# A scan's last 64 state channels in six TensorE passes instead of ten: weight halves side by side, sums added afterwards

## The chip, the cores and the metric

The kernel runs on one core of one Trainium2 chip. The metric is the device time of one execution in microseconds (us). Three runs of the kernel before took 5264.43, 5264.77 and 5265.05 us; the median is 5264.77 us.

## The reference, cut to what matters

A feature map x of 16 images, 56 by 56 positions, 192 channels, goes through two residual blocks. The first one concerns us: the group-normalized map is cut into 7x7 windows, normalized per token (layer norm 1), and run through a linear recurrence over the 49 tokens of each window; its states are mixed, normalized again (layer norm 2), and sent through a two-layer MLP with a GELU between.

```python
xB = xw @ Bm                      # xw: windows x 49 tokens x 192 channels
def step(h, xb):
    h = xb + h @ A                # A: 192 x 192
    return (h, h)
_, hs = jax.lax.scan(step, h0, swapaxes(xB, 0, 1))
w = swapaxes(hs, 0, 1) @ Cm
y = _ln(w, ln2_w, ln2_b)
y = gelu(y @ W1 + b1) @ W2 + b2   # W1: 192 x 768, W2: 768 x 192
x = x + w + y
```

The second block is windowed attention. It follows when the first block is done and the change does not touch it.

## The kernel before, in words

**Precision.** A float32 product is made of products of a narrower type: each operand is split into an upper part, rounded to that type, and a lower part, the remainder. The class `Split` (L81 on) holds four tiles for one weight matrix: `a_hi`, `a_lo` for input channels 0 to 127 and `b_hi`, `b_lo` for input channels 128 to 191. The b tiles have those 64 rows twice, because the data's second half keeps its upper part in partitions 0 to 63 and its lower part in partitions 64 to 127. So one product with 192 input channels is five matmuls (`Split.terms`): a_hi with upper and lower data, a_lo with upper data, b_hi and b_lo with both.

**Stages.** A preamble reads x for the group statistics and prepares the weights (L164 on ScalarE writes the upper parts, L176 on GpSimd the lower ones). Then comes the scan stage with the first block; then the attention.

**The scan stage.** It has 98 steps: 49 window positions (t) by two chunks (c) of 4 x 128 windows. Every engine runs the same `slot(t, c)` with its own part, several steps at once. With n = 2t + c, in slot n

- SyncE (SP) issues the load of x for step n+2 into `xt` (L352), then waits until `s_x1` says that the first block's output of step n-1 is complete (L360), and issues its 14 stores (L380). SP issues everything in this order, one after the other.
- TensorE (PE) does the scan of step n+1 (L619: `ps_h` gets ten passes for channels 0 to 127, then ten for channels 128 to 191, 512 columns each), the transposes of y of step n (L590, L592), the second half of the MLP's second layer of step n-1 (L604), the first MLP layer of step n (L635; it waits for the lower parts of y through `s_yl`), the mixing with C of step n+1 (L646), the transposes of the normalized x of step n+2, and the first half of the second layer of step n (L604).
- ScalarE (ACT) writes the upper parts of h (L402, two instructions, bias included), of y (L391, L392), the GELU (L416), the upper parts of the hidden layer (L421) and of xn.
- VectorE (DVE) starts its slot with group norm on `xt` for step n+2 (L501, L503), and waits there for the load. Then it writes the lower parts of h of step n+1 (L482, two instructions), the lower parts of y of step n (L480, two), and adds the second half of the MLP's output of step n-1 into x1 (L489, L492), which gives `s_x1`. The rest of the slot follows: statistics, g_lo, normalizations, the first half of x1.
- GpSimd (POOL) makes the residual, two powers, two of the g_lo pieces and the running sums.

Within one engine the order is written out by hand; across engines there are only semaphores. The head of the DVE slot, whose order matters below, is

```python
dve.wait_ge(s_x[c], 16 * (t + 2))
dve.tensor_tensor(xn[c][:, :, :], xt[c][:, :, :], R1[:, r, :], ALU.mult).then_inc(s_gs, 1)
dve.tensor_tensor(xn[c][:, :, :], xn[c][:, :, :], M1[:, r, :], ALU.subtract).then_inc(s_gn, 1)
dve.wait_ge(s_hh, n + 2)
lower_parts(h_hi[1 - c], h_lo[1 - c], ps_h, hbias).then_inc(s_hl, 1)
dve.wait_ge(s_yh, n + 1)
lower_parts(y_hi, y_lo, ps_g).then_inc(s_yl, 1)
dve.wait_ge(s_w2, n)
x1_half(1 - c, 1, s_xb, n).then_inc(s_x1, 1)
```

Of the kernel before, what the change touches and what calls it, by code (L numbers as in the profile page):

```python
# [8 lines left out]
f32r = mybir.dt.float32r  # L9
ALU = mybir.AluOpType  # L10
ACT = mybir.ActivationFunctionType
# [3 lines left out]
IMGS, SIDE, C = 16, 56, 192  # L15
# [8 lines left out]
P = 128  # L24
CB = C - P
# [4 lines left out]
NTOK = TPC * P  # L30
# [25 lines left out]
def build(nc, x, A, Bm, Cm, ln1, ln2, W1, b1, W2, b2,  # L56
# [3 lines left out]
    def sem(name):  # L60
        return top.enter_context(nc.semaphore(name))

    with top:
# [17 lines left out]
        class Split:  # L81
# [1 line left out]

            def __init__(self, ctx, name, cols):
                self.parts = [ctx.enter_context(nc.sbuf_tensor(f"{name}_{k}", [P, cols], f32r))
                              for k in ("a_hi", "a_lo", "b_hi", "b_lo")]

            def terms(self, data_hi, data_lo, cols, pick=lambda t: t):  # L90

# [5 lines left out]
        with ExitStack() as ctx:  # L97
            def sb(name, shape, dt=fp32, where=ctx):
                return where.enter_context(nc.sbuf_tensor(name, shape, dt))
# [3 lines left out]

            R1 = sb("R1", [P, NT, C])
            M1 = sb("M1", [P, NT, C])
            W_B, W_A, W_C = (Split(ctx, name, C) for name in ("wB", "wA", "wC"))
            W_1 = Split(ctx, "w1", HID)
            w2 = sb("w2", [P, FT, 2, C], f32r)
            b2b = sb("b2b", [P, C])
# [1 line left out]
            hbias = sb("hbias", [P, 2])  # L111
# [4 lines left out]
            with ExitStack() as pre:  # L116
# [14 lines left out]
                ps_g, ps_h = ps("ps_g0", [P, 512], where=pre), ps("ps_h0", [P, 512], where=pre)  # L131
# [18 lines left out]
                @block.scalar  # L150
                def _(act):
                    for dst, src in ((ident[:, :], identity), (img_mean[:, :], image_mean),
                                     (raw_2[:, :, :], W2.rearrange("(f p) n -> p f n", p=P)),
                                     (b2b[:, :], b2.partition_broadcast(P)),
                                     (l1[:, :, :], ln1), (l2[:, :, :], ln2), (b1c[:, :], b1)):
                        act.dma_start(dst, src).then_inc(s_w, 16)
                    for raw, src in ((raw_B, Bm), (raw_A, A), (raw_C, Cm), (raw_1, W1)):
                        act.dma_start(raw[:, :, :], src.rearrange("(k p) n -> p k n", p=P)).then_inc(s_w, 16)

                    act.wait_ge(s_fold, 1)  # L160
                    for full, parts in ((fold_B, W_B), (raw_A, W_A), (raw_C, W_C), (fold_1, W_1)):
                        for t in range(2):
                            act.activation(parts.parts[2 * t][:, :], full[:, t, :], ACT.Copy)
                    act.activation(w2[:, :, 0, :], raw_2[:, :, :], ACT.Copy).then_inc(s_wh, 1)  # L164

                @block.gpsimd
                def _(pool):
                    pool.memset(acc_x[:, :, :], 0.0)
                    pool.memset(acc_x2[:, :, :], 0.0)
                    pool.memset(neg_half[:, :], -0.5).then_inc(s_i0, 1)  # L170
                    pool.wait_ge(s_i0, 1)

                    pool.wait_ge(s_wh, 1)
                    for full, parts in ((fold_B, W_B), (raw_A, W_A), (raw_C, W_C), (fold_1, W_1)):
                        for t in range(2):
                            pool.tensor_tensor(parts.parts[2 * t + 1][:, :], full[:, t, :],  # L176
                                               parts.parts[2 * t][:, :], ALU.subtract)
                    pool.tensor_tensor(w2[:, :, 1, :], raw_2[:, :, :], w2[:, :, 0, :], ALU.subtract)

                    pool.wait_ge(s_fold, 11)  # L180
                    pool.tensor_tensor(gtab[:, 0, :, :], gvar[:, :, :],
                                       neg_half[:, :].rearrange("p (a b) -> p a b", a=2), ALU.pow).then_inc(s_pow, 1)
# [96 lines left out]
            xn_lo = [sb(f"xn_lo{b}", [P, NTOK], f32r) for b in range(2)]  # L279
            h_hi = [sb(f"h_hi{b}", [P, 2, NTOK], f32r) for b in range(2)]  # L280
            h_lo = [sb(f"h_lo{b}", [P, NTOK], f32r) for b in range(2)]
            yb = sb("yb", [P, TPC, C])
            y_hi, y_lo = sb("y_hi", [P, 2, NTOK], f32r), sb("y_lo", [P, NTOK], f32r)
            gF = [sb(f"gF{b}", [P, NTOK]) for b in range(4)]
# [28 lines left out]
            s_st1, s_ag1, s_ve1 = sem("ln1_stats"), sem("ln1_aggregated"), sem("ln1_var_eps")  # L313
            s_rs1, s_xn = sem("ln1_rstd"), sem("xn_ready")
            s_t1, s_xh, s_xl = sem("xn_transposed"), sem("xn_hi_ready"), sem("xn_lo_ready")
            s_scan, s_hh, s_hl = sem("scan_summed"), sem("h_hi_ready"), sem("h_lo_ready")
            s_cm, s_res, s_rsum = sem("mixed"), sem("residual_ready"), sem("residual_summed")
            s_st2, s_ag2, s_ve2 = sem("ln2_stats"), sem("ln2_aggregated"), sem("ln2_var_eps")
            s_rs2, s_y = sem("ln2_rstd"), sem("y_ready")
# [66 lines left out]
            @block.scalar  # L386
            def _(act):
                act.wait_ge(s_init, 1)

                def upper_parts(hi, full):  # L390
                    act.activation(hi[:, 0, :], full[:, 0, :], ACT.Copy)  # L391
                    return act.activation(hi[0:CB, 1, :], full[0:CB, 1, :], ACT.Copy)  # L392

                def slot(t, c):
                    n = CHUNKS * t + c
                    if there(n + 1):

                        d = 1 - c
                        act.wait_ge(s_scan, n + 2)
                        upto(act, s_cm, n)  # L400
                        for k, rows in enumerate((P, CB)):
                            last = act.activation(h_hi[d][0:rows, k, :], ps_h[0:rows, k, :], ACT.Identity,  # L402
                                                  bias=hbias[0:rows, k:k + 1])
                        last.then_inc(s_hh, 1)
                    if there(n):
                        act.wait_ge(s_t2, n + 1)
                        upper_parts(y_hi, ps_g).then_inc(s_yh, 1)
                    if there(n):
                        for f in range(FT):
                            act.wait_ge(s_w1, FT * n + f + 1)  # L410
                            if f == 0:
                                upto(act, s_w2, n)
                            elif f >= 4:

                                act.wait_ge(s_gld, len(LO_DVE) * n + LO_DVE.index(f - 4) + 1)
                            act.activation(gF[f % 4][:, :], ps_g[:, f % 2, :], ACT.Gelu,  # L416
                                           bias=b1f[:, f:f + 1]).then_inc(s_gelu, 1)

                            for g in range(max(f - 1, 0), f + (f == FT - 1)):
                                act.wait_ge(s_gelu, FT * n + g + 1)  # L420
                                act.activation(g_hi[:, g, :], gF[g % 4][:, :], ACT.Copy).then_inc(s_gh, 1)  # L421
                    if there(n + 2):
                        act.wait_ge(s_t1, n + 3)
                        upto(act, s_scan, n + 1)
                        upper_parts(xn_hi[c], ps_h).then_inc(s_xh, 1)

                slots(act, slot)
# [44 lines left out]

            @block.vector
            def _(dve):
                def lower_parts(hi, lo, full, bias=None):

                    for k, rows, dst in ((0, P, lo[:, :]), (1, CB, hi[CB:P, 1, :])):
                        src, up = full[0:rows, k, :], hi[0:rows, k, :]
                        if bias is None:
                            last = dve.tensor_tensor(dst, src, up, ALU.subtract)  # L480
                        else:
                            last = dve.scalar_tensor_tensor(out=dst, in0=src, scalar=bias[0:rows, k:k + 1], in1=up,  # L482
                                                            op0=ALU.add, op1=ALU.subtract)
                    return last

                def x1_half(b, half, partial, count):
# [7 lines left out]
                def slot(t, c):  # L494
# [9 lines left out]
                                          ALU.subtract).then_inc(s_gn, 1)  # L504
                    if there(n + 1):

                        dve.wait_ge(s_hh, n + 2)
                        lower_parts(h_hi[1 - c], h_lo[1 - c], ps_h, hbias).then_inc(s_hl, 1)
                    if there(n):
                        dve.wait_ge(s_yh, n + 1)  # L510
                        lower_parts(y_hi, y_lo, ps_g).then_inc(s_yl, 1)
# [72 lines left out]
            def _(pe):  # L584
# [23 lines left out]
                def slot(t, c):  # L608
                    n = CHUNKS * t + c
                    if there(n + 1):  # L610

                        d = 1 - c
                        pe.wait_ge(s_xl, n + 2)
                        upto(pe, s_hl, n)
                        for m, rows in enumerate((P, CB)):
                            cols = slice(P * m, P * m + rows)
                            terms = (*W_B.terms(xn_hi[d], xn_lo[d], cols), *W_A.terms(h_hi[d], h_lo[d], cols))
                            for k, (w, v) in enumerate(terms):
                                last = pe.matmul(ps_h[0:rows, m, :], w, v, start=(k == 0), stop=(k == len(terms) - 1))  # L619
                        last.then_inc(s_scan, 1)  # L620
                    if there(n):
                        pe.wait_ge(s_y, n + 1)
# [703 lines left out]
```

## Time and profile before

| | |
|---|---|
| runs of the kernel | 5264.43, 5264.77, 5265.05 us |
| span of the profiled execution, first to last instruction | 5261.6 us |
| median of the runs less this span | 3.2 us |
| preamble | up to about 160 us |
| scan stage, first to last L619 matmul | 167 to 2382 us |
| steps in the scan stage | 98 |

The profile is of one execution; its own time is its span of 5261.6 us and about 3 us around it, as the runs have. Times in rows are us from the span's start unless marked ns. PE is TensorE's matmuls, PEld its weight loads, SPq SyncE's queue, which issues the DMAs.

### The profile page before, as it was taken

To read this page: it belongs to the slowest core of one execution; us is meant where nothing else is said; L and a number is where in the kernel's file an instruction comes from. 1 tells how busy PE (TensorE), PEld (TensorE's weight loads), DVE (VectorE), ACT (ScalarE), POOL (GpSimd) and SP (SyncE) were. 2 spreads that over 40 slices of the span, in tenths; PEclk is the share of its full clock that TensorE was granted. 3 is DMA by queue.
4 is the path that set the end of the run, shared out by engine and by line. 5 is a ranking of instruction groups with operands and counts; after the bars stand their busy time and mean duration, and the time that the engine had idled before them with its cause. 6 is when DMAs were issued, how large, how long until landed. Compare 5 with 4: busy or idle time off the path is not lost.

```text
span 5261.6 us, 134580 instructions
## 1 busy us (share of the span) xinstructions
PE 5043.1 (96%) x48584; PEld 4492.2 (85%) x48584; DVE 4296.8 (82%) x8359; ACT 2931.9 (56%) x5618; POOL 2646.9 (50%) x1717
## 2 busy tenths in 40 slices
PE   0699999999999999996999999999999999999999
PEld 0588888888888888885999999999999999999998
DVE  6788888888888888884777777777777777777777
ACT  0244444444444444442766666666666666666666
POOL 0245555555545554554555555555555555555554
PEclk9999999999999999997999999999999999999999
DMA  7011111111111111111111111111111111111111
GB/s 309 26 38 39 39 41 38 39 39 40 41 37 39 39 41 38 39 39 43 35 37 36 38 39 36 36 36 36 39 37 36 39 38 36 36 36 37 39 36 32
DMA packets 254250, 233.59 MB, mean 44 GB/s; under 512 B 19836, under 2 KB 252492, under 8 KB 253004
## 3 DMA queue, kind: packets, MB, share of 16 engines
q1 hardware_dynamic: 251460, 230.74, 14.8%
q10 hardware_dynamic: 2736, 2.14, 0.1%
q8 instruction: 33, 0.54, 0.0%
q14 instruction: 21, 0.16, 0.0%
HBM read 145.48 MB, written 87.33 MB: 44 GB/s over the span
## 4 chain that ended last, share of the span: by engine, by line
PE 53%; DMA 0%; DVE 0%; POOL 0%; ACT 0%; issue 0%; SPq 0%; ACTq 0%; DVEq 0%
PE ps_s L1195 18%; PE ps_t L1205 8%; PE ps_w L1143 7%; PE ps_w L1175 7%; PE ps_w L1156 5%; PE ps_v L1233 5%; PE ps_w L1130 2%; DMA mask<-in_shift_mask 0%; PE ps_s L1112 0%; PE ps_s L1113 0%; POOL E L860 0%; DVE L L1067 0%; DVE mx L1071 0%; DVE bias L1017 0%; DVE sm L1075 0%
## 5 line engine op out<-in xcount | busy, mean ns | idle before, releaser
L860 POOL TENSOR_TENSOR E<-E,ri 128x588 f32<-128x588 f32 x512 | 809.5, 1581 | 1271.3 <-DVE ri L1077 1271.3
L1195 PE MATMUL ps_s<-Kp,Qm 128*64 128x98 f32 x12288 | 1001.6, 250 | 0.0
L1195 PEld LDWEIGHTS ps_s<-Kp,Qm 128*64 128x64 f32 x12288 | 903.4, 135 | 67.2 <-issue 49.8
L945 ACT ACTIVATE PT<-ps_t 128x768 f32<-128x768 f32 x512 | 414.0, 809 | 643.2 <-PE ps_t L1205 643.2
L1067 DVE SCALAR_TENSOR_TENSOR L<-ps_s,bias 128x588 f32<-128x588 f32 x512 | 394.3, 770 | 408.3 <-PE ps_s L1195 408.2
L604 PE MATMUL ps_o<-w,g_hi 128*128 128x384 f32 x2352 | 709.9, 365 | 5.9 <-DVE g_lo L544 4.1
L416 ACT ACTIVATE gF<-ps_g,b1f 128x512 f32<-128x512 f32 x588 | 404.9, 689 | 394.0 <-PE ps_g L635 391.8
L604 PE MATMUL ps_o<-w,g_lo 128*128 128x192 f32 x2352 | 534.4, 254 | 0.0
L402 ACT ACTIVATE h_hi<-ps_h,hbias 128x512 fp32r<-128x512 f32 x196 | 123.1, 679 | 702.6 <-PE ps_h L619 702.6
L443 POOL TENSOR_TENSOR res<-xt,b2b 128x768 f32<-128x768 f32 x98 | 180.8, 1845 | 591.1 <-DVE x L492 591.1
L604 PEld LDWEIGHTS ps_o<-w,g_hi 128*128 128x128 f32 x2352 | 429.1, 189 | 26.6 <-issue 24.8
L1205 PE MATMUL ps_t<-ident,E 128*128 128x128 f32 x3072 | 447.7, 282 | 0.8 <-POOL E L860 0.7
L604 PEld LDWEIGHTS ps_o<-w,g_lo 128*128 128x128 f32 x2352 | 443.4, 191 | 0.0
L1071 DVE TENSOR_REDUCE mx<-L 128x12 f32<-128x588 f32 x512 | 392.1, 766 | 17.6
L1175 PE MATMUL ps_w<-wp,oT 128*128 128x192 f32 x2048 | 388.3, 333 | 0.7 <-ACT oT L964 0.7
L1075 DVE TENSOR_REDUCE sm<-E 128x12 f32<-128x588 f32 x512 | 386.2, 754 | 0.0
L1205 PEld LDWEIGHTS ps_t<-ident,E 128*128 128x128 f32 x3072 | 326.7, 140 | 63.4 <-POOL E L860 1.7
L1080 DVE TENSOR_TENSOR L<-L,mx 128x588 f32<-128x588 f32 x512 | 362.1, 707 | 0.0
L936 ACT ACTIVATE E<-L 128x588 f32<-128x588 f32 x512 | 357.7, 699 | 4.0 <-DVE L L1080 0.7
L421 ACT ACTIVATE g_hi<-gF 128x512 fp32r<-128x512 f32 x588 | 355.3, 621 | 0.0
L453 POOL TENSOR_TENSOR g_lo<-gF,g_hi 128x512 fp32r<-128x512 f32 x196 | 250.5, 1298 | 198.5 <-ACT g_hi L421 198.5
L1175 PEld LDWEIGHTS ps_w<-wp,oT 128*128 128x128 f32 x2048 | 326.3, 190 | 9.3 <-ACT oT L964 0.8
(208 smaller groups left out, 13082.4 us busy)
## 6 DMA issues: line engine op xcount, KB each, us to landing
xs<-in_x SPq DMA_DIRECT2D x8, 4704.0 KB, 22.6
xt<-in_x SPq DMA_DIRECT2D x98, 384.0 KB, 3.4
x_cells<-x SPq DMA_DIRECT2D x784, 48.0 KB
xb<-x_cells SPq DMA_DIRECT2D x256, 147.0 KB
out<-yo SPq DMA_DIRECT2D x256, 147.0 KB
gnr<-gn_rows SPq DMA_DIRECT2D x128, 192.0 KB
x_cells<-x SPq DMA_DIRECT2D x392, 24.0 KB
x_cells<-x SPq DMA_DIRECT2D x196, 3.0 KB
```

Source lines behind the costliest of these rows:

```text
L416: act.activation(gF[f % 4][:, :], ps_g[:, f % 2, :], ACT.Gelu, bias=b1f[:, f:f + 1]).then_inc(s_gelu, 1)
L604: last = pe.matmul(dst, g[:, f, P * k:P * (k + 1)], w, start=(f == 0 and i == 0), stop=(f == FT - 1 and i == 1))
L860: pool.tensor_tensor(e, e, ri[p][:, :].unsqueeze(2).to_broadcast([P, HEADS, T]), ALU.mult)\
L945: act.activation(PT[lp % 2][:, :, :].rearrange("p (a b) q -> p a (b q)", a=2), ps_t[:, :, 0:JB * P], ACT.Copy).then_inc(s_ptc, 1)
L1067: dve.scalar_tensor_tensor(out=L[p][:, :, :].rearrange("p (a h) m -> p a (h m)", a=2), in0=ps_s[:, :, 0:HEADS // 2 * T], scalar=HD ** -0.5 ...
L1071: dve.tensor_reduce(mx[p][:, :], L[p][:, :, :], AX.X, ALU.max).then_inc(s_mx, 1)
L1075: dve.tensor_reduce(sm[pp][:, :], E[pp][:, :, 0:T], AX.X, ALU.add).then_inc(s_sm, 1)
L1080: dve.tensor_tensor(L[p][:, :, :], L[p][:, :, :], mx[p][:, :].unsqueeze(2).to_broadcast([P, HEADS, T]), ALU.subtract).then_inc(s_sub, 1)
L1143: last = pe.matmul(ps_w(QK + m)[:, 0:NW * TE].rearrange("p (w t) -> p w t", t=TE), w, x, start=(k == 0), stop=(k == len(terms) - 1))
L1175: last = pe.matmul(ps_w(OUT1 if half else OUT0)[:, C * a:C * (a + 1)], oT[d][p][:, k, :, :].rearrange("p w t -> p (w t)"), wp[:, k, :], st ...
L1195: last = pe.matmul(ps_s[SLOT * w:SLOT * (w + 1), j // JB, 2 * T * (j % JB):2 * T * (j % JB + 1)], Qm[c][:, j, 2 * p + w, :], Kp[c][:, j // ...
L1205: last = pe.transpose(ps_t[:, j // JB, P * (j % JB):P * (j % JB + 1)], E[lp][:, 2 * j:2 * j + 2, :].rearrange("p h m -> p (h m)"), ident[: ...
```

## The change

The scan's second group of output channels, 128 to 191, used 64 of the 128 columns of the stationary operand. Now the tiles `a_hi` and `b_hi` of B and A get 64 more columns, into which the lower weight parts of these channels are written as well. A pass with columns 128 to 255 of such a tile gives the product with the upper weights in partitions 0 to 63 of `ps_h[:, 1]` and that with the lower weights in partitions 64 to 127. `packed_terms` lists three passes per matrix instead of five, so there are 10 + 6 passes in a step instead of 10 + 10.

The two halves must be added, and one instruction reads the accumulators of both halves at different partitions, so it goes by steps: ScalarE copies the lower half to `h_low` in SBUF; VectorE adds the upper half, bias and `h_low` into `h_b`; ScalarE rounds `h_b` to the upper part of h; VectorE makes the lower parts. Two semaphores are new: `s_hc` (h_low copied) and `s_hb` (h_b summed).

```diff
-            W_B, W_A, W_C = (Split(ctx, name, C) for name in ("wB", "wA", "wC"))
+            W_B, W_A = (Split(ctx, name, C, CB) for name in ("wB", "wA"))
+            W_C = Split(ctx, "wC", C)
...
+            def packed_terms(self, data_hi, data_lo):
+                both = slice(self.cols - self.beside, self.cols + self.beside)
+                a_hi, _, b_hi, _ = self.parts
+                return ((a_hi[:, both], data_hi[:, 0, :]), (a_hi[:, both], data_lo[:, :]), (b_hi[:, both], data_hi[:, 1, :]))
...
                     for full, parts in ((fold_B, W_B), (raw_A, W_A), (raw_C, W_C), (fold_1, W_1)):
                         for t in range(2):
-                            pool.tensor_tensor(parts.parts[2 * t + 1][:, :], full[:, t, :],
-                                               parts.parts[2 * t][:, :], ALU.subtract)
+                            pool.tensor_tensor(parts.lower(t), full[:, t, :], parts.upper(t), ALU.subtract)
+                            if parts.beside:
+                                pool.tensor_tensor(parts.lower_beside(t), full[:, t, P:C], parts.upper(t)[:, P:C],
+                                                   ALU.subtract)
...
                         act.wait_ge(s_scan, n + 2)
                         upto(act, s_cm, n)
-                        for k, rows in enumerate((P, CB)):
-                            last = act.activation(h_hi[d][0:rows, k, :], ps_h[0:rows, k, :], ACT.Identity,
-                                                  bias=hbias[0:rows, k:k + 1])
-                        last.then_inc(s_hh, 1)
+                        act.activation(h_low[0:CB, :], ps_h[CB:P, 1, :], ACT.Copy).then_inc(s_hc, 1)
+                        act.activation(h_hi[d][:, 0, :], ps_h[:, 0, :], ACT.Identity, bias=hbias[:, 0:1])
+                        act.wait_ge(s_hb, n + 2)
+                        act.activation(h_hi[d][0:CB, 1, :], h_b[0:CB, :], ACT.Copy).then_inc(s_hh, 1)
...
+                        d = 1 - c
+                        dve.wait_ge(s_hc, n + 2)
+                        dve.scalar_tensor_tensor(out=h_b[0:CB, :], in0=ps_h[0:CB, 1, :], scalar=hbias[0:CB, 1:2],
+                                                 in1=h_low[0:CB, :], op0=ALU.add, op1=ALU.add).then_inc(s_hb, 1)
                         dve.wait_ge(s_hh, n + 2)
-                        lower_parts(h_hi[1 - c], h_lo[1 - c], ps_h, hbias).then_inc(s_hl, 1)
+                        dve.scalar_tensor_tensor(out=h_lo[d][:, :], in0=ps_h[:, 0, :], scalar=hbias[:, 0:1],
+                                                 in1=h_hi[d][:, 0, :], op0=ALU.add, op1=ALU.subtract)
+                        dve.tensor_tensor(h_hi[d][CB:P, 1, :], h_b[0:CB, :], h_hi[d][0:CB, 1, :],
+                                          ALU.subtract).then_inc(s_hl, 1)
...
-                        for m, rows in enumerate((P, CB)):
-                            cols = slice(P * m, P * m + rows)
-                            terms = (*W_B.terms(xn_hi[d], xn_lo[d], cols), *W_A.terms(h_hi[d], h_lo[d], cols))
+                        first = slice(0, P)
+                        for m, terms in enumerate(((*W_B.terms(xn_hi[d], xn_lo[d], first),
+                                                    *W_A.terms(h_hi[d], h_lo[d], first)),
+                                                   (*W_B.packed_terms(xn_hi[d], xn_lo[d]),
+                                                    *W_A.packed_terms(h_hi[d], h_lo[d])))):
                             for k, (w, v) in enumerate(terms):
-                                last = pe.matmul(ps_h[0:rows, m, :], w, v, start=(k == 0), stop=(k == len(terms) - 1))
+                                last = pe.matmul(ps_h[:, m, :], w, v, start=(k == 0), stop=(k == len(terms) - 1))
                         last.then_inc(s_scan, 1)
```

## Rows read from the trace of the kernel before

**Rows 1.** The page: span, busy us, share of the span, instructions of each engine.

```profile
span 5261.6 us, 134580 instructions
...
PE 5043.1 (96%) x48584; PEld 4492.2 (85%) x48584; DVE 4296.8 (82%) x8359; ACT 2931.9 (56%) x5618; POOL 2646.9 (50%) x1717
```

**Rows 2.** Waits of 400 to 2290 us, SP's queue too: us, times, longest.

```profile
DVE xn L501 <- DMA xt<-in_x: 74.9, 83, 1.2
...
SPq L360 <- DVE x L492: 779.0, 83, 9.4
```

**Rows 3.** Timeline of SP's queue: start us, us, engine, line, what.

```profile
1033.68 0.43 SPq L352 DMA_DIRECT2D xt<-in_x  x1
1044.60 11.28 SPq L380 DMA_DIRECT2D x_cells<-x  x14
1056.59 0.44 SPq L352 DMA_DIRECT2D xt<-in_x  x1
```

**Rows 4.** Timeline of DVE, head of one slot; in brackets idle before and releaser.

```profile
1036.98 1.39 DVE L501 TENSOR_TENSOR xn<-xt,R 128x768 f32<-128x768 f32 x1 [0.71 <-DMA xt<-in_x]
1038.40 0.96 DVE L503 TENSOR_TENSOR xn<-xn,M 128x768 f32<-128x768 f32 x1
1039.37 0.75 DVE L482 SCALAR_TENSOR_TENSOR h_lo<-ps_h,hbias,h_hi 128x512 fp32r<-128x512 f32 x1
1040.13 0.74 DVE L482 SCALAR_TENSOR_TENSOR h_hi<-ps_h,hbias,h_hi 64x512 fp32r<-64x512 f32 x1
1040.91 0.69 DVE L480 TENSOR_TENSOR y_lo<-ps_g,y_hi 128x512 fp32r<-128x512 f32 x1
1041.62 0.68 DVE L480 TENSOR_TENSOR y_hi<-ps_g,y_hi 64x512 fp32r<-64x512 f32 x1
1042.39 0.56 DVE L489 TENSOR_TENSOR x<-ps_o,res 128x384 f32<-128x384 f32 x1
1042.98 0.56 DVE L492 TENSOR_TENSOR x<-ps_o,x 128x384 f32<-128x384 f32 x1
```

**Rows 5.** Timeline of PE in the same step: scan's narrow passes, last L604, first L635.

```profile
1035.60 0.39 PE L619 MATMUL ps_h<-xn_hi,wB_a_hi 128*64 128x512 f32 x1
...
1037.65 0.39 PE L619 MATMUL ps_h<-h_hi,wA_b_lo 128*64 128x512 f32 x1
...
1041.99 0.36 PE L604 MATMUL ps_o<-w,g_hi 128*128 128x384 f32 x1
1042.36 0.50 PE L635 MATMUL ps_g<-y_hi,w_a_hi 128*128 128x512 f32 x1
```

**Rows 6.** PEld groups of 400 to 2290 us: busy us, mean ns, then idle before.

```profile
L635 PEld LDWEIGHTS ps_g<-y_hi,w_a_hi 128*128 128x128 f32 x498 | 93.1, 187 | 44.9 <-DVE y_hi L480 20.9
...
L619 PEld LDWEIGHTS ps_h<-xn_hi,wB_a_hi 128*128 128x128 f32 x83 | 15.9, 192 | 0.0
```

**Rows 7.** Timeline of ACT in the same step.

```profile
1038.08 1.25 ACT L402 ACTIVATE h_hi<-ps_h,hbias 128x512 fp32r<-128x512 f32 x2 [7.14 <-PE ps_h L619]
1039.23 0.58 ACT L391 ACTIVATE y_hi<-ps_g 128x512 fp32r<-128x512 f32 x1
1039.71 0.59 ACT L392 ACTIVATE y_hi<-ps_g 64x512 fp32r<-64x512 f32 x1
1043.82 0.69 ACT L416 ACTIVATE gF<-ps_g,b1f 128x512 f32<-128x512 f32 x1 [3.52 <-PE ps_g L635]
```

**Rows 8.** ACT groups of 400 to 2290 us: busy us, mean ns, then idle before.

```profile
L421 ACT ACTIVATE g_hi<-gF 128x512 fp32r<-128x512 f32 x498 | 300.9, 621 | 0.0
...
L402 ACT ACTIVATE h_hi<-ps_h,hbias 64x512 fp32r<-64x512 f32 x83 | 55.7, 671 | 0.0
...
L392 ACT ACTIVATE y_hi<-ps_g 64x512 fp32r<-64x512 f32 x83 | 48.5, 584 | 0.0
```

**Rows 9.** The source view of L176 on POOL (min/median/max ns), and a wait of the whole span.

```profile
L176 POOL TENSOR_TENSOR wB_a_lo<-fold_B,wB_a_hi x1: 589/589/589, 94.7 to 94.7; 128x192 fp32r<-128x192 f32 x1
...
POOL gtab L181 <- DVE gvar L228: 39.5, 1, 39.5
```

**Rows 10.** Stretches at the scan's start: busy us of PE, PEld, DVE, ACT, POOL, then PEclk.

```profile
172.00:178.80 6.80, 3.91 (x25) 2.66 (x23) 2.96 (x10) 1.25 (x2) 0.00 (x0) 1.00 0.00 0
178.80:189.10 10.30, 6.65 (x24) 5.26 (x23) 7.54 (x23) 1.07 (x2) 3.79 (x3) 0.50 0.14 41
```

**Rows 11.** Timeline of PE there: the one long wait within the first stretch.

```profile
177.26 0.36 PE L646 MATMUL ps_r<-wC_a_hi,h_hi 128*128 128x192 f32 x1 [2.89 <-DVE h_hi L482]
```

More of the change, by code:

```diff
@@ L81, in build, with __init__, upper, lower @@
         class Split:
-            def __init__(self, ctx, name, cols):
-                self.parts = [ctx.enter_context(nc.sbuf_tensor(f"{name}_{k}", [P, cols], f32r))
+            def __init__(self, ctx, name, cols, beside=0):
+                self.cols, self.beside = cols, beside
+                self.parts = [ctx.enter_context(nc.sbuf_tensor(f"{name}_{k}", [P, cols + beside * (k[-1] == "i")], f32r))
                               for k in ("a_hi", "a_lo", "b_hi", "b_lo")]
+            def upper(self, t):
+                return self.parts[2 * t][:, 0:self.cols]
+            def lower(self, t):
+                return self.parts[2 * t + 1][:, :]
+            def lower_beside(self, t):
+                return self.parts[2 * t][:, self.cols:self.cols + self.beside]
+            def packed_terms(self, data_hi, data_lo):
+                both = slice(self.cols - self.beside, self.cols + self.beside)
+                a_hi, _, b_hi, _ = self.parts
+                return ((a_hi[:, both], data_hi[:, 0, :]), (a_hi[:, both], data_lo[:, :]), (b_hi[:, both], data_hi[:, 1, :]))
             def terms(self, data_hi, data_lo, cols, pick=lambda t: t):
@@ L162, in _ @@
                         for t in range(2):
-                            act.activation(parts.parts[2 * t][:, :], full[:, t, :], ACT.Copy)
+                            act.activation(parts.upper(t), full[:, t, :], ACT.Copy)
                     act.activation(w2[:, :, 0, :], raw_2[:, :, :], ACT.Copy).then_inc(s_wh, 1)
@@ L281, in build @@
             h_lo = [sb(f"h_lo{b}", [P, NTOK], f32r) for b in range(2)]
+            h_low, h_b = sb("h_low", [P, NTOK]), sb("h_b", [P, NTOK])
             yb = sb("yb", [P, TPC, C])
@@ L315, in build @@
             s_t1, s_xh, s_xl = sem("xn_transposed"), sem("xn_hi_ready"), sem("xn_lo_ready")
-            s_scan, s_hh, s_hl = sem("scan_summed"), sem("h_hi_ready"), sem("h_lo_ready")
+            s_scan, s_hc, s_hb, s_hh, s_hl = sem("scan_summed"), sem("h_b_low_copied"), sem("h_b_summed"), sem("h_hi_ready"), sem("h_lo_ready")
             s_cm, s_res, s_rsum = sem("mixed"), sem("residual_ready"), sem("residual_summed")
@@ L474, in _, with lower_parts @@
             def _(dve):
-                def lower_parts(hi, lo, full, bias=None):
+                def lower_parts(hi, lo, full):
                     for k, rows, dst in ((0, P, lo[:, :]), (1, CB, hi[CB:P, 1, :])):
[L478 to L483, printed above, removed]
+                        last = dve.tensor_tensor(dst, full[0:rows, k, :], hi[0:rows, k, :], ALU.subtract)
                     return last
```

## Prediction

> **What bounds the kernel now.** The page comes first: TensorE is busy 96% of the span, VectorE 82% [rows 1]. That reads as a kernel bound by its matmuls, of which the change removes some. But busy shares cannot tell a full engine from one that is paced by something of nearly the same length, so I read who waits for whom in the steady part of the scan stage. There VectorE begins every slot by waiting for the load of x, 74.9 us in 83 steps or 0.90 us a step; no other wait appears at its slot's head. SyncE in turn waits 779.0 us for VectorE's L492 before it may store [rows 2]. These two waits face each other, and the timeline shows that they form a ring.
>
> Follow one turn. SyncE issues the load at 1033.68 [rows 3]; VectorE starts L501 at 1036.98, 3.30 us later. It then runs L501, L503, the two lower parts of h, the two of y, L489 and L492 with gaps under 0.1 us and ends at 1042.98 + 0.56 = 1043.54 [rows 4]: 6.56 us. That end releases SyncE: the first store goes out at 1044.60, 1.06 us later, the 14 stores take 11.28 us, and 0.71 us behind them the next load is issued at 1056.59, because it stands behind them in the queue [rows 3]. 3.30 + 6.56 + 1.06 + 11.28 + 0.71 = 22.91 us, which is exactly the time between the two loads. Nobody in this ring waits for anybody outside it, but for at most 0.06 us before L489, where VectorE is free at 1042.30 and starts at 1042.39 [rows 4].
>
> TensorE turns with the ring, but it is the one that waits: before L635 its weight load waits 20.9 us in 83 steps for VectorE's lower part of y, 0.25 us a step [rows 6]. That lower part is a piece of the ring. So **the ring sets the step**, TensorE follows with little slack, and what the change does to VectorE between L503 and L492 counts in full.
>
> **The change, part by part.** *Four passes fewer.* The ten narrow passes start between 1035.60 and 1037.65 [rows 5]: 2.05 / 9 = 0.228 us apiece. A pass with 128 stationary columns needs a longer weight load, 192 ns [rows 6], still under the 228. Four passes less end the scan 0.91 us earlier in each step. In the ring this is worth nothing: the lower parts of h start when L503 ends, at 1039.36, and the upper parts were ready at 1038.08 + 1.25 = 1039.33 [rows 4, 7]. They would be ready earlier, and VectorE would still be in L503. The 0.91 us turn into a longer wait before L635. They also end L604 earlier, which takes away the 0.06 us before L489.
>
> *ScalarE's copy of h_low.* It starts at the scan's end and takes about 0.58 us like L392 [rows 8]. Here the earlier scan helps: it ends near 1037.2 instead of 1038.08, the copy near 1037.8, and L503 at 1039.36. Hidden by the wait for the load and by L501 and L503; with the cover gone it would cost its 0.6 us. L402 for channels 0 to 127 is hidden behind it in the same way.
>
> *VectorE's sum h_b.* A new instruction in the ring, of the form of the second L482 (64x512, one operand from PSUM): 0.74 us and 0.02 for the gap [rows 4].
>
> *The new round trip.* Behind h_b VectorE waits until ScalarE has rounded h_b; h_lo, which does not need it, stands behind the same wait. No row shows this 64x512 copy from SBUF. The nearest are 584 ns (64x512, from PSUM) and 621 ns (128x512, from SBUF) [rows 8]; I take 0.60, with 0.55 and 0.69 as ends (the latter is somewhat over the 671 of L402). A handover costs 0.06 us from VectorE (1042.30 to L635 at 1042.36 [rows 4, 5]) and 0.04 back (ScalarE's 1039.33 to 1039.37 [rows 4, 7]). Sum 0.70 us, between 0.60 and 0.90 if both handovers are doubled. Queued behind ScalarE's wait are the upper parts of y; they take 0.59 + 0.48 = 1.07 us [rows 7] and VectorE needs them only after h_lo and the lower part, 0.75 + 0.70 later than the handover. Hidden, by 0.4 us. The GELU behind them waits 3.52 us for TensorE anyway [rows 7].
>
> *h's lower part* becomes a plain subtraction, 0.68 like L480 for 0.74: minus 0.06 [rows 4].
>
> *Preamble.* Four subtractions on GpSimd, at most 0.59 us each as their wider sisters take; GpSimd later waits 39.5 us for VectorE [rows 9]. Nothing.
>
> No DMA is added or moved. Nothing else on the ring changes: L501 meets GpSimd's running sums as before, since both are paced from the same end of the lower y.
>
> **The sum.** 0.76 + 0.70 - 0.06 - 0.06 = 1.34 us a turn (1.24 to 1.54 with the ends). The load is waited for in 92 of the 98 steps (83 of them in the steady stretch, one each [rows 2]; the others are at the ends, where the shorter scan and the longer handover about cancel). 92 x 1.34 = 123 us on the span of 5261.6 [rows 1]; the runs lie 3.2 us above that span, so 5264.8 + 123 = **5388 us**. With the ends of the unknown: 5379 to 5406.
>
> **Rivals.** *TensorE's clock falls* (slower still). TensorE's wait before L635 grows to 0.25 + 0.91 + 1.34 = 2.5 us a step. Near the start of the stage it waited 2.89 us once, at full clock [rows 11], and 1.5 us after it resumed the granted clock went from 1.0 to 0.5, from 2.4 to 1.2 GHz, for 10.3 us [rows 10]. The Trainium skill ("TensorE: Matmul & The Clock Gate", section What's actually happening) says why: "the default state is throttled, and activity releases the throttle"; by that rule this longer wait can cost clock, and the trace agrees once, for a longer wait. Each L635 pass would then take about twice its 0.23 us for some 15 passes, so TensorE loses perhaps 1.7 us. VectorE has 0.90 us before the load lands to absorb it; 0.8 us would reach the ring. A late TensorE has a shorter wait in the next step, so I count every other step: 0.4 x 92 = 37 us, 5425 us. Against it: 2.5 is under 2.89, and no row shows such a wait at a steady pace.
>
> *TensorE paces after all* (faster). If the ring had 1.3 us of slack that the turn above hides, TensorE would set the step through its own chain: scan end, h, y, L635. Before, from 1038.04 to 1042.30, 4.26 us [rows 4, 5]. After: 0.62 (h_low) + 0.80 (h_b) + 0.64 + 0.77 + 0.70 + 0.71 + 0.70 = 4.94. So 0.68 longer for 0.91 saved, -0.23 x 98 = -23 us: 5242 us. It decides wherever the load lands 1.3 us before VectorE asks for it; all 83 waits say it lands late [rows 2].
>
> The Trainium skill ("Perfetto Trace Analysis", section Identifying the Most-Contended Engine) would have the engine with the highest occupancy taken as the bound, with weight-load share as TensorE's measure: 85% here, still the highest [rows 1]. By that rule all of 0.91 x 98 = 89 us is gained, 5176 us; the waits of rows 2 and 6 disagree, since TensorE is the one that waits.
>
> *The ring absorbs it* (same). If part of SyncE's 11.28 us were itself a wait for earlier transfers, a later start would shorten it by as much. The stores come out evenly and SyncE idles 9.4 us a step before them [rows 2], so little speaks for it: 5265 us.
>
> **How the numbers follow.** The ring with the clock kept 0.52, with a falling clock 0.34, TensorE pacing 0.07 (its pure form included), absorbed 0.05, and 0.02 for something slower that I don't see. Chances: faster 0.07, same 0.05, slower 0.88, where 0.2% of 5265 is about 10 us, what a measurement of this kernel can tell from no change. The range takes in both ring cases and their ends: 5370 (1.15 us a turn) to 5440.
>
> **What would show it.** Right: a step of about 24.1 us; VectorE still waiting about 0.9 us for the load in each; about 0.7 us a step of VectorE waiting for ScalarE's h_hi; TensorE's wait before L635 near 2.5 us; SyncE's stores still 11.3 us. Half-clock stretches after these waits would show the second case. Wrong: loads that land before VectorE asks, a step under 22.8 us, or stores issued faster.

## Result and profile after

The changed kernel takes **5520.9 us** (median of 4 runs, 5519.58 to 5525.6) against 5264.91 us (4 runs, 5264.43 to 5265.34) for the kernel before: a ratio of 1.0489, 95% interval 1.0475 to 1.0503. I had forecast 5388 us, with 5440 as the upper end. The direction is right; the size is 133 us short.

Lines have moved: L501 is now L517, L503 L519, L482 is h_b L525, h_lo L528 and h_hi L530, L480 L499, L489 and L492 are L505 and L508, L532 L555, L619 L644, L635 L660, L604 L627; SyncE's load is L373 and its stores L401. The page of the changed kernel, to be read beside [rows 1]:

```profile
span 5518.9 us, 133996 instructions
...
PE 5088.2 (92%) x48192; PEld 4570.3 (83%) x48192; DVE 4435.5 (80%) x8457; ACT 3000.1 (54%) x5716; POOL 2645.6 (48%) x1721
```

TensorE has 392 matmuls fewer (4 in each of 98 steps), yet is busy for longer, 5088 us for 5043. Less work in more busy time means that each matmul took longer. The windows say why; columns as in [rows 10], the last but two being the granted clock:

```profile
215.00:360.00 145.00, 132.48 (x790) 117.70 (x789) 127.32 (x266) 66.10 (x115) 68.72 (x48) 1.00 0.14 38
400.00:1400.00 1000.00, 913.19 (x5083) 802.09 (x5081) 846.93 (x1718) 432.46 (x745) 449.42 (x314) 0.93 0.13 35
1006.56:1009.30 2.74, 2.74 (x7) 2.16 (x8) 2.57 (x11) 0.20 (x1) 1.47 (x1) 0.50 0.00 0
```

From 215 to 360 us the scan runs at full clock, from 400 us on at a mean of 0.93: with two levels, 1.2 and 2.4 GHz, (1 - 0.93) / 0.5 is 14% of the time at the lower one, or some 3.6 us of each step of 25.60. The third row is one such stretch, and TensorE's timeline shows where it lies:

```profile
1006.56 0.79 PE L660 MATMUL ps_g<-y_hi,w_a_hi 128*128 128x512 f32 x1 [2.17 <-DVE y_hi L499]
1007.15 0.63 PE L660 MATMUL ps_g<-y_lo,w_a_hi 128*128 128x512 f32 x1
1007.58 0.63 PE L660 MATMUL ps_g<-y_hi,w_a_lo 128*128 128x512 f32 x1
...
1009.90 0.40 PE L660 MATMUL ps_g<-y_hi,w_b_hi 128*128 128x512 f32 x1
1010.14 0.40 PE L660 MATMUL ps_g<-y_hi,w_b_lo 128*128 128x512 f32 x1
```

TensorE waits 2.17 us for the lower part of y, and resumes at half clock: passes start 0.43 us apart (1007.15 to 1007.58), 0.24 later on. It is the start of the first MLP layer, on which ScalarE's GELU and VectorE's g_lo depend.

The waits of the steady stretch (400 to 2290 us, 74 steps; us, times, longest), SP's queue last:

```profile
DVE g_lo L555 <- ACT g_hi L442: 197.2, 146, 2.1
PEld ps_g L660 <- DVE y_hi L499: 183.5, 74, 2.5
...
SPq L381 <- DVE x L508: 902.6, 74, 12.2
```

VectorE's wait for the load, 0.90 us a step in [rows 2], is not among them. TensorE's wait before the first layer is 183.5 / 74 = 2.48 us, forecast near 2.5. The one that grew is at L555: 197.2 / 74 = 2.66 us a step, 1.13 at the same place (L532) of the kernel before, in the same stretch:

```profile
DVE g_lo L532 <- ACT g_hi L421: 94.1, 166, 0.7
```

SyncE idles 12.2 us a step for 9.4: its stores cannot be what grew. VectorE's slot head, beside [rows 4]:

```profile
1024.17 0.56 DVE L508 TENSOR_TENSOR x<-ps_o,x 128x384 f32<-128x384 f32 x1
1024.65 2.17 DVE L517 TENSOR_TENSOR xn<-xt,R 128x768 f32<-128x768 f32 x1
...
1027.73 0.74 DVE L525 SCALAR_TENSOR_TENSOR h_b<-ps_h,hbias,h_low 64x512 f32<-64x512 f32 x1
1029.17 0.75 DVE L528 SCALAR_TENSOR_TENSOR h_lo<-ps_h,hbias,h_hi 128x512 fp32r<-128x512 f32 x1 [0.70 <-ACT h_hi L425]
1029.93 0.69 DVE L530 TENSOR_TENSOR h_hi<-h_b,h_hi 64x512 fp32r<-64x512 f32 x1
```

h's part is as forecast: 0.74 for h_b, 0.70 for the round trip, 0.69 for the lower part. But L517 starts right behind L508 and takes 2.17 us (mean 2.12), 1.20 in the kernel before. GpSimd and SyncE's queue in the same step say why:

```profile
1022.34 1.86 POOL L487 TENSOR_TENSOR acc_x<-acc_x,x 128x768 f32<-128x768 f32 x1
1024.14 1.87 POOL L490 TENSOR_TENSOR acc_x<-acc_x,x1sq 128x768 f32<-128x768 f32 x1
```

```profile
1008.97 11.37 SPq L401 DMA_DIRECT2D x_cells<-x  x14
1020.60 0.43 SPq L373 DMA_DIRECT2D xt<-in_x  x1
```

The load goes out at 1020.60; with the 3.30 us of [rows 3, 4] it lands near 1023.9, before VectorE asks at 1024.65. So VectorE no longer waits, and L517 begins while GpSimd is still in the last of its sums (1024.14 to 1026.01). L517 ends at 1026.82, 0.81 us after that: about the 0.95 us that it takes where none of the sums runs beside it (e5 below).

The first steps of the same trace ran otherwise, as I had forecast them:

```profile
320.37 11.38 SPq L401 DMA_DIRECT2D x_cells<-x  x14
...
344.67 11.45 SPq L401 DMA_DIRECT2D x_cells<-x  x14
...
368.60 11.36 SPq L401 DMA_DIRECT2D x_cells<-x  x14
...
394.48 11.37 SPq L401 DMA_DIRECT2D x_cells<-x  x14
...
419.83 11.28 SPq L401 DMA_DIRECT2D x_cells<-x  x14
```

Up to 368.60 the steps are 24.3 and 23.9 us, behind it 25.9 and 25.4. **One execution shows the forecast step while the clock is full and the longer one once it falls.**

### The profile page after: what moved, and what is told of

Same layout as the page of the kernel before. It is cut to its first block, busy times and chain, and to the rows that moved or that the text cites. A ratio compares the mean times of both kernels' runs of the same rounds, so it can differ in the third digit from the quotient of the medians.

```text
span 5518.9 us, 133996 instructions
## 1 busy us (share of the span) xinstructions
PE 5088.2 (92%) x48192; PEld 4570.3 (83%) x48192; DVE 4435.5 (80%) x8457; ACT 3000.1 (54%) x5716; POOL 2645.6 (48%) x1721
## 4 chain that ended last, share of the span: by engine, by line
PE 50%; DMA 0%; DVE 0%; POOL 0%; ACT 0%; issue 0%; SPq 0%; ACTq 0%; DVEq 0%
PE ps_s L1220 17%; PE ps_t L1230 7%; PE ps_w L1168 7%; PE ps_w L1200 6%; PE ps_w L1181 5%; PE ps_v L1258 4%; PE ps_w L1155 2%; DMA mask<-in_shift_mask 0%; PE ps_s L1137 0%; PE ps_s L1138 0%; POOL E L885 0%; DVE L L1092 0%; DVE mx L1096 0%; DVE bias L1042 0%; DVE sm L1100 0%
## 5 line engine op out<-in xcount | busy, mean ns | idle before, releaser
L627 PE MATMUL ps_o<-w,g_hi 128*128 128x384 f32 x2352 | 710.0, 365 | 5.9 <-DVE g_lo L567 4.1
L627 PE MATMUL ps_o<-w,g_lo 128*128 128x192 f32 x2352 | 534.5, 254 | 0.0
L660 PE MATMUL ps_g<-y_hi,w_a_hi 128*128 128x512 f32 x588 | 280.3, 477 | 215.5 <-DVE y_hi L499 215.5
L627 PEld LDWEIGHTS ps_o<-w,g_hi 128*128 128x128 f32 x2352 | 429.3, 189 | 26.3 <-issue 24.4
L627 PEld LDWEIGHTS ps_o<-w,g_lo 128*128 128x128 f32 x2352 | 443.6, 191 | 0.0
L422 ACT ACTIVATE h_low<-ps_h 64x512 f32<-64x512 f32 x98 | 58.4, 596 | 613.5 <-PE ps_h L644 613.5
```

The lines of the kernel that those rows point to most:

```text
L627: last = pe.matmul(dst, g[:, f, P * k:P * (k + 1)], w, start=(f == 0 and i == 0), stop=(f == FT - 1 and i == 1))
```

## Experiments

A step is read from SyncE's load issues between 1000 and 2000 us of the profiled execution: first, last, and the steps between.

| kernel | us (interval of the ratio to before) | loads from, to, steps | step us |
|---|---|---|---|
| before | 5264.91 | 1011.02, 1990.98, 43 | 22.79 |
| changed | 5520.9 (1.0475 to 1.0503) | 1020.60, 1993.41, 38 | 25.60 |
| e1: changed, wait filled | 5392.18 (1.0223 to 1.0257) | 1008.71, 1997.46, 41 | 24.12 |
| e2: changed, four passes back | 5393.26 (1.0225 to 1.026) | 1010.69, 1999.70, 41 | 24.12 |
| e3: changed, load first | 5518.5 (1.0464 to 1.0499) | 1008.32, 1981.06, 38 | 25.60 |
| e4: before, load first | 5266.21 (0.999 to 1.0009) | 999.78, 1980.71, 43 | 22.81 |
| e5: changed, sums later | 5522.69 (1.0473 to 1.0508) | 1020.03, 1992.84, 38 | 25.60 |
| e6: changed, y first | 5314.46 (1.0076 to 1.0109) | 1003.79, 1984.49, 42 | 23.35 |
| e8: e6, load first, sums later | 5362.09 (1.0167 to 1.0201) | 1020.22, 1976.63, 40 | 23.91 |
| e9: before, the edits of e8 | 5295.67 (1.0039 to 1.0073) | 1011.46, 1983.13, 42 | 23.14 |
| e10: e6, h behind statistics | **5194.2** (0.9849 to 0.9882) | 1004.70, 1999.17, 45 | 22.10 |
| e11: before, the order of e10 | 5283.25 (1.0021 to 1.0047) | 1016.54, 1983.93, 42 | 23.03 |

### Does the clock make the difference? (e1, e2)

e1 fills TensorE's wait with ten passes whose result nobody reads; e2 puts the four saved passes back, as useless ones, at the head of the second scan group. Both add work to the changed kernel and take none away.

```diff
 pe (e1)
+    for _ in range(10):
+        pe.matmul(ps_r[:, 0, :], W_1.upper(0)[:, 0:P], ..., start=True, stop=True)
     pe.wait_ge(s_yl, n + 1)
 pe (e2), second group only
+    for w, v in terms[0:4]:
+        pe.matmul(ps_h[:, m, :], w, v, start=True, stop=True)
     for k, (w, v) in enumerate(terms):
```

> The changed kernel with ten useless passes of 512 columns (10 x 0.229 = 2.29 us) put where TensorE waits 2.2 us a step for the lower part of y. Clock theory: the wait is what halves TensorE's clock in every step; late first-layer passes make VectorE's slot late, and L517 late into GpSimd's sums. With the wait filled the granted clock in the scan stage stays 1.0, the load of x is again what VectorE waits for, and the step is 22.8 + 1.35: 5262 + 92 x 1.35 + 3 = about 5390 us, faster with more work. Rival, round trip alone: the clock is a companion, the added VectorE and ScalarE steps and the overlap with GpSimd make up the 256 us; then the time stays at 5521 us.

> The changed kernel with four useless passes at the head of the second group, so that TensorE's scan takes as long as before and only the round trip for h_b remains. Clock theory: the wait before the first layer shrinks from 2.5 to about 1.6 us; if such a wait still halves the clock, about 5500 us, if not, about 5390 us, which would say that the saved passes themselves cost 130 us. Round trip alone: 5521 us.

More work, 129 us and 128 us less time. The window and the waits of e1 (78 steps):

```profile
400.00:1400.00 1000.00, 1000.00 (x5814) 879.87 (x5813) 867.42 (x1827) 455.47 (x785) 477.84 (x333) 1.00 0.14 37
```

```profile
DVE g_lo L555 <- ACT g_hi L442: 93.8, 156, 0.8
DVE xn L517 <- DMA xt<-in_x: 61.4, 78, 1.1
DVE h_lo L528 <- ACT h_hi L425: 54.6, 78, 0.7
PEld ps_g L664 <- DVE y_hi L499: 25.8, 78, 0.4
```

and the group of its first product (busy us, mean ns, idle before):

```profile
L517 DVE TENSOR_TENSOR xn<-xt,R 128x768 f32<-128x768 f32 x78 | 101.3, 1298 | 61.4 <-DMA xt<-in_x 61.4
```

The clock is at 1.00 and the ring through the load is back. Its step is 24.12 us, 1.33 above the kernel before; the forecast's sum was 1.34. e2's scan also ran at 1.00, with this wait before the first layer:

```profile
PEld ps_g L662 <- DVE y_hi L499: 121.8, 78, 1.6
```

With 1.56 us in every step the clock stayed; with 2.48 us in every step it fell. So **the saved passes cost 128 us**: with them put back, even as useless ones, the wait is short enough here for the clock to stay.

How the 1.48 us between e1 and the changed kernel come about, from waits and groups of both: the wait at L555 grows from 93.8 / 78 = 1.20 to 2.66 us (+1.46, the first layer at half clock); the wait for the load goes (-0.79); L517 is stretched from 1.30 to 2.12 (+0.83). Sum 1.50. The slack ahead of the load absorbed half of the clock's cost, and the stretch beside GpSimd gave it back.

### Does the load still matter? (e3, e4)

SyncE issues the stores of a slot one slot later, behind the next load. e4 does the same to the kernel before.

```diff
 sp
-    if there(n - 1):
-        d, u = (1 - c), (t if c else t - 1)
+    if there(n - 2):
+        d, u = c, t - 1
         ...
-        sp.wait_ge(s_x1, n)
+        sp.wait_ge(s_x1, n - 1)
```

> The changed kernel with SyncE's stores issued one slot later, behind the load, so that the load of x no longer stands behind 14 stores. The prediction's ring of load and stores, if it still set the step: a gain of 100 us and more. Clock theory: in the changed kernel VectorE no longer waits for the load, so nothing moves: 5510 to 5530 us.

> The kernel before with the same edit. If the ring of load and stores alone set its step of 22.8 us, TensorE's work is next at about 22.4 us: 5265 - 96 x 0.4 = 5227 us. If VectorE's L501, started earlier, is stretched by GpSimd's running sums as in the changed kernel (2.1 for 1.2 us), the 0.9 us are given back: 5260 to 5270 us.

In the changed kernel almost nothing moves (2.4 us): the load's ring no longer sets its step. In the kernel before nothing moves either, and that speaks against my account of it. VectorE no longer waits for the load there, and its busy time rises from 885 to 923 of 1000 us; the group of e4's first product:

```profile
L502 DVE TENSOR_TENSOR xn<-xt,R 128x768 f32<-128x768 f32 x82 | 174.0, 2122 | 0.9
```

From 1.20 to 2.12 us: what VectorE had waited it now spends beside the sums. The kernel before had at least two rings of the same length, the load's and VectorE's own with a stretched first product. A third candidate is TensorE itself: its matmuls leave next to no gap in either kernel (busy 999.92 of 1000 us before, 999.81 in e4, from 400 to 1400 us), and neither run tells it from the rings.

### Is it the sums that stretch L517? (e5)

GpSimd's three sums wait until the next slot's L519 has run, so that none stands beside L517.

```diff
 pool
     pool.wait_ge(s_x1, n)
+    if there(n + 3):
+        pool.wait_ge(s_gn, n + 4)
```

> The changed kernel in which GpSimd starts its three running sums only when VectorE has done L519 of the next slot, so that they no longer run beside L517. Overlap theory: L517 falls from 2.12 to about 0.96 us; the clock still falls, so about 1.15 us of the 25.6 us step go and the time is near 5521 - 85 x 1.15 = 5420 us, with the load of x waited for again. Rival: L517 is slow for another reason (the load's data arriving beside it); it stays at 2.1 us and the time at 5521 us.

The groups of e5 (its lines are two further down):

```profile
L532 DVE TENSOR_TENSOR h_hi<-h_b,h_hi 64x512 fp32r<-64x512 f32 x74 | 136.7, 1847 | 1.0
...
L519 DVE TENSOR_TENSOR xn<-xt,R 128x768 f32<-128x768 f32 x74 | 70.6, 954 | 8.4 <-DMA xt<-in_x 7.8
```

The first product falls to 0.954 us, so the sums were its cause. But the sums now stand beside h_hi's difference, which rises from 0.685 to 1.847: 1.17 saved, 1.16 lost. h_b and h_lo between them stay at 0.74 and 0.75. Those read PSUM; the two that were stretched read both operands from SBUF. The Trainium skill ("SBUF — State Buffer", section Who interferes with whom) says the same: a VectorE instruction with two SBUF inputs contends with a GpSimd instruction that reads SBUF. The trace agrees, with these numbers.

### Can the order be mended? (e6, e8, e9)

y's lower parts first on VectorE, then h_b and the second half of x1, then h's lower parts (e6). e8 adds the edits of e3 and e5; e9 makes the edits of VectorE, SyncE and GpSimd on the kernel before, where ScalarE still writes h's upper parts ahead of y's.

```diff
 dve (e6)
+    lower_parts(y_hi, y_lo, ps_g)
     h_b = ps_h + bias + h_low
-    h_lo, h_hi lower parts
-    lower_parts(y_hi, y_lo, ps_g)
     x1_half(1 - c, 1, s_xb, n)
+    h_lo, h_hi lower parts
 act (e6)
+    upper_parts(y_hi, ps_g)
     h_hi[0:CB, 1] = h_b
-    upper_parts(y_hi, ps_g)
```

> The changed kernel with VectorE and ScalarE doing y first: only h_b stays between L519 and the second half of x1, h's lower parts come behind it. Ring theory: TensorE's wait before the first layer shrinks to well under 1 us, the clock stays at 1.0, and the step is set by VectorE's own slot with L517 at 2.1 us, some 22.4 us: 5230 us. If the clock alone mattered and the ring not, the time would be that of the filled wait, 5390 us.

> The changed kernel with y first, the stores one slot behind the load, and GpSimd's sums behind L519. Then nothing but TensorE's own work should set the step, 22.35 - 0.91 = 21.4 us: 5265 - 96 x 1.35 = about 5135 us. If VectorE's slot still sets it, 5200 us or more.

> The kernel before, ten and ten passes, with the same three edits. If TensorE sets the step in both, it is 22.35 us here and the time is 5265 - 96 x 0.4 = 5225 us, some 90 us more than with six passes; if VectorE or a transfer sets it, both kernels come out alike.

All three came out above what theory gave. e6 does take most of the loss back, and its clock stays at 1.00. But VectorE is then busy 960 of 1000 us, with these groups, and this wait of TensorE's transposes:

```profile
L518 DVE TENSOR_TENSOR xn<-xt,R 128x768 f32<-128x768 f32 x81 | 171.1, 2113 | 0.8
...
L541 DVE TENSOR_TENSOR h_hi<-h_b,h_hi 64x512 fp32r<-64x512 f32 x81 | 148.8, 1837 | 1.1
```

```profile
PEld ps_h L617 <- DVE xn L564: 115.0, 81, 1.5
```

h_hi's difference now runs beside GpSimd's residual and is stretched again, and with h_lo it stands ahead of the statistics of xn, so xn is late for TensorE. In e8 the same wait is 1.46 us a step, and a late scan delays y as well:

```profile
DVE y_lo L503 <- ACT y_hi L414: 131.0, 80, 2.8
PEld ps_h L620 <- DVE xn L567: 115.5, 79, 2.1
```

Part of its scan is at half clock (mean 0.98). In e9 VectorE's wait for y_hi alone is 176.5 / 82 = 2.15 us: it asks for y first, and ScalarE makes it behind h. My expectations had counted what each edit took off one path, and not what it moved onto another.

### A version that beats both (e10, e11)

h's two lower parts go behind the statistics, ahead of VectorE's first g_lo (L555): where VectorE stood idle for ScalarE, and GpSimd takes only its powers.

```diff
 dve (e10, on e6)
-    h_lo, h_hi lower parts
     bn_stats, bn_aggr, vea
+    h_lo, h_hi lower parts
     g_lo of LO_DVE[:2]
```

> The changed kernel with y's lower parts first on VectorE, h_b behind them, and h's lower parts behind the statistics of xn, just ahead of the first of VectorE's g_lo, where VectorE now stands idle 2.1 us for ScalarE and GpSimd has only the powers to take. Theory (the step is the ring through VectorE's slot: y's lower parts, first layer, GELU, g_lo, and back): with y first alone VectorE was busy 960 of 1000 us and h_hi's difference took 1.84 us beside GpSimd's residual; here it should fall back to about 0.69 us and stand in idle time, so a step of 22.3 to 22.8 us and 5220 to 5265 us, with the granted clock at 1.00 through the scan. Rival 1: the difference is only stretched somewhere else and xn is still late for TensorE's transposes (a wait of 1 to 2 us a step ahead of them): near the 5314 us of y first alone. Rival 2: h's lower parts are now late for the mix, which waits for them, and the clock falls again: above 5400 us.

> The same placing of h's lower parts in the kernel before: y's lower parts and the second half of x1 first, h's lower parts behind the statistics. Theory: the kernel before is held at 22.9 us by two rings of nearly one length (the load ring, and VectorE's slot with the stretched first product); this edit takes 1.4 us off the way from y to the load in both, so TensorE paces the step at about 22.4 us: 5215 to 5240 us. Rival 1: h_hi's difference or xn is late for TensorE, a wait ahead of the transposes or the mix takes the gain: 5265 to 5300 us. Rival 2: TensorE was the bound all along: 5262 to 5267 us.

e10 takes **5194.2 us, 0.9865 of the kernel before** (0.9849 to 0.9882), below what theory expected. The waits of e10, the group of h_hi's difference, its window and TensorE ahead of the first layer:

```profile
DVE xn L518 <- DMA xt<-in_x: 61.8, 86, 1.2
PEld ps_o L632 <- issue: 38.1, 86, 0.4
PEld ps_h L618 <- DVE xn L565: 10.1, 37, 0.3
```

```profile
L554 DVE TENSOR_TENSOR h_hi<-h_b,h_hi 64x512 fp32r<-64x512 f32 x85 | 58.2, 685 | 1.1
```

```profile
400.00:1400.00 1000.00, 989.80 (x5894) 881.48 (x5894) 939.82 (x1994) 500.87 (x864) 522.66 (x362) 1.00 0.15 40
```

```profile
1012.34 0.36 PE L632 MATMUL ps_o<-w,g_hi 128*128 128x384 f32 x1
1012.54 0.39 PE L665 MATMUL ps_g<-y_hi,w_a_hi 128*128 128x512 f32 x1
```

h_hi's difference is at 0.685 us, the wait for ScalarE ahead of the first g_lo, 2.66 us a step in the changed kernel, has no row in this list, and the first MLP layer (L665) follows the matmuls ahead of it without a gap. The waits of TensorE in this list make (38.1 + 10.1) / 86 = 0.56 us a step: it is nearly full. But VectorE waits for the load in every step again (61.8 / 86 = 0.72 us), and the load's ring closes, here from the load that SyncE issued at 1004.70:

```profile
1008.31 1.39 DVE L518 TENSOR_TENSOR xn<-xt,R 128x768 f32<-128x768 f32 x1 [0.70 <-DMA xt<-in_x]
...
1013.39 0.56 DVE L509 TENSOR_TENSOR x<-ps_o,x 128x384 f32<-128x384 f32 x1
```

```profile
1015.01 11.29 SPq L401 DMA_DIRECT2D x_cells<-x  x14
1027.00 0.44 SPq L373 DMA_DIRECT2D xt<-in_x  x1
```

That is 3.61 us to L518, 5.64 to the end of L509 with no gap over 0.04 us between VectorE's instructions, 1.06 to the first store, 11.29 for the stores and 0.70 to the next load: 22.30 us, the whole turn (22.10 in the mean). VectorE's part is shorter than the 6.56 us of [rows 4], since h's lower parts have left it. So the ring and TensorE have nearly the same length in e10; no run tells which of them holds it at 22.10.

e11 gives VectorE the same order in the kernel before, with all ten passes; ScalarE keeps its own there, h's upper parts ahead of y's. It became *slower* than the kernel before (theory had said 5215 to 5240). Its waits:

```profile
DVE y_lo L480 <- ACT y_hi L392: 80.5, 82, 1.0
DVE x L489 <- PE ps_o L604: 55.9, 82, 0.7
DVE xn L501 <- DMA xt<-in_x: 55.7, 82, 1.0
PEld ps_o L604 <- issue: 36.7, 82, 0.4
```

Two waits are new on VectorE: 0.98 us a step for y's upper part and 0.68 for TensorE's second layer ahead of x1. Both lie within the load's ring, which therefore waits for ScalarE and TensorE and doesn't hold the step by itself. TensorE waits 36.7 / 82 = 0.45 us a step at L604, and nowhere near as long anywhere else: with ten passes the matmuls fill nearly all of the 23.03 us, so the order could win little. The two kernels differ in step by 23.03 - 22.10 = 0.93 us, and in time by 89 us: the four passes at 0.228 us are 0.91 us a step and 89 us in 98. TensorE is busy 990 of 1000 us in e10 and 989 in e11, from 400 to 1400 us. **Where TensorE is nearly full, the saved passes are worth about all they cost.** VectorE's order alone gains nothing. What it would gain with y first on ScalarE too stays open, because e11 left that out.

## Why the prediction was wrong

*The direction and the ring.* h_b (0.76 forecast; 0.74 and a gap), the round trip (0.70; 54.6 / 78 = 0.70) and the shorter difference (0.68; 0.685) were right, and so was their sum as long as the clock stayed: 123 us forecast, 126 and 127 measured in e1 and e2 against the 5265.85 us of the kernel before, measured beside them, with 24.12 us for the "about 24.1" of a step. Four passes fewer bring the ring nothing: right, and TensorE's wait came out as forecast at 2.5.

*What failed* is the choice between that case and the rival "TensorE's clock falls", and above all that rival's price. I had its mechanism and place, and set against it that 2.5 us is under the 2.89 of [rows 11]. The clock fell all the same. Two of its terms were mis-sized:

- "I count every other step". After 368 us it fell in every step. The alternation was an argument without a row behind it: y is late in every step because VectorE's slot is long, and TensorE's lateness adds to that slot.
- "VectorE has 0.90 us before the load lands to absorb it". It did absorb 0.79 us, but the line "L501 meets GpSimd's running sums as before, since both are paced from the same end of the lower y" fell: once VectorE doesn't wait for the load, L517 starts beside the sums and takes 0.83 us longer. The rival's 1.7 us lost by TensorE measured 1.46 at L555; I let 0.8 reach the ring in half the steps, 0.4 us; 1.48 reached it in each.

0.4 x 92 = 37 us were forecast for the clock, 5520.9 - 5392.2 = 129 us measured (e1).

*"The ring sets the step, TensorE follows with little slack."* The first half is too strong. e4 takes the load out of the ring and leaves the time as it was; what else had the same length (VectorE's slot, TensorE's matmuls) could not be seen in a wait, because only the last of several releasers shows. That had no part in the miss, since y and h lie in both rings.

*"TensorE paces after all"* had 0.07 and its conditions were rightly judged unfulfilled here. e10 and e11 show what the matmuls are worth once the order brings TensorE close to full.

*The signs I had named.* SyncE's stores still took 11.3 us and the wait for h_hi was 0.7. The wait for the load, named as the sign of a right step, vanished: by my own list, "loads that land before VectorE asks" meant wrong.

## What to carry to other kernels

Work taken from an engine that waits anyway lengthens its wait, and on TensorE that wait can cost the clock in every step: fill the wait as a test, since a kernel that gets faster with useless matmuls has named its cause. Where several rings have nearly the same length, slack in one is not free: ask what the early instruction will then run beside. Before giving up a saving, look for a place in the order where the new instructions meet idle time of their engine and of its neighbour; here the same saving went from +4.9% to -1.3% by where three of VectorE's instructions (h_b and h's two lower parts) and ScalarE's copy of h_b stand.

## What the runs showed of the hardware

- A wait of TensorE of about 2.5 us in every step of 25.6 us came with half clock for a few us behind each; 1.56 us in every step (e2) did not. The length of the wait alone does not decide it. In the changed kernel's own first steps, 215 to 360 us, six such waits made 14.0 us, 2.3 each, and the clock stayed at 1.00. In e3 six waits made 14.9 us between 327 and 490 us, eight made 19.8 us between 494 and 700 us, 2.5 each in both stretches; the clock was full in the first and fell in the second:

```profile
327.20:490.00 162.80, 149.44 (x894) 132.94 (x894) 145.95 (x293) 74.67 (x130) 77.68 (x54) 1.00 0.14 38
494.50:700.00 205.50, 187.69 (x1043) 164.84 (x1042) 174.05 (x355) 89.03 (x153) 92.56 (x65) 0.93 0.13 35
```

  What else it takes, and why the fall begins only at about 368 us in the changed kernel, stays open. The Trainium skill ("TensorE: Matmul & The Clock Gate", section What's actually happening) has activity release the throttle, and the rows agree in the direction; what they add is that one wait of 2.5 us a step can cost the clock in every step.
- The changed kernel, e3 and e5 have the same step of 25.60 us to two decimals between 1000 and 2000 us, though L517 takes 2.12 us in two and 0.95 in the third. That the falls of the clock hold the step at this length would explain it, and e3 fits that: its loads from 351.56 to 496.25 us, at full clock, are 24.1 us apart. But no run here tells it, for e5, from the chance that h_hi's stretch just made up for L517's.
- Two SBUF operands on VectorE beside GpSimd's elementwise work: 0.95 became 2.12 us for 128x768, 0.685 became 1.85 for 64x512, both times about 1.17 us more; with an operand from PSUM, no change.
